# Spreading dt and u by broadcast reads, drives on GpSimd, decay in PSUM and half-row scans in a Mamba, attention and expert kernel

## The chip, the cores and the metric

The kernel runs on one core of a Trainium2 chip. The metric is the device time of one execution in microseconds, the median of several; less is better. Engines are named as in the profile: PE is TensorE, DVE VectorE, ACT ScalarE, POOL GpSimd, SP SyncE, which here only issues transfers.

## The reference

For each of 8 batches (64 channels, T = 1024 tokens) three layers follow each other: a selective scan (Mamba) with group norm and residual, causal attention of 8 heads of width 8, and a mixture of 8 experts, of which each token takes two. The part that the change is about:

```python
dt = jax.nn.softplus(dt_low @ W_dt + b_dt)      # [B, T, 128]
dA = jnp.exp(dt_t[..., None] * A)               # A: 128 x 16 states
dBx = dt_t[..., None] * B_t[:, None, :] * x_t[..., None]
h = dA * h + dBx                                # a recurrence over the 1024 tokens
y = jnp.einsum('bdn,bn->bd', h, C_t)
...
att = jnp.einsum('bqhd,bkhd->bhqk', q, k) * scale   # then causal softmax, times v
```

## The kernel before

A software pipeline runs over the batches. `pipeline` (L466) calls each engine's `program` for 12 turns, here turn 0 to 11; in a turn each part works on another batch: `c` the first half of the Mamba layer, `p` its end and the q and k projection, `b` the attention, `f` its projection and the experts. A full turn, with all of them, is turn 4 to 8. The order of each engine's work is written out by hand. Batches wait for each other by counting semaphores (`Signal`, L29).

A turn has two phases. The **score phase** is `for s in range(NSCORE)`: 48 steps of q times k (L1198, plus a mask product L1202) into two pairs of PSUM banks, and a row maximum on DVE over each (L926), so that the softmax can subtract it. q and k stand as three bf16 parts, so a product contracts 72 rows: `q_stack[0:9 * DH]`. Between these steps, at numbers in the tables `beside`, stands the dense work of `c` and `p`: the projections (L1106), the last folds of the scan, norms.

The **round phase** is `for s, units, turns in ROUNDS`: 28 rounds. From the fifth on each round has one of 24 attention steps: 4 products of k and q (`weigh`, 75 rows: the row maximum comes in as three more rows), 4 exponentials on ACT (L801), and the products with v (`add_values`). `TURNS` puts the experts of `f` into the rounds. `UNITS_IN` puts the scan of `c` there.

The scan has the 128 channels x 16 states as 16 chunks of 128 rows (8 channels times 16 states), each 1024 tokens long. Each chunk needs dt and u = dt * x of its 8 channels on 128 rows. Before, ACT and POOL split both into three bf16 parts in the score phase (`high`, `mid`, `less_high`, `less_mid`; L728, L732, L627, L632), SP copies them into `dt_rows` and `u_rows`, and PE replicates them with a 0/1 matrix, half a row at a time, into PSUM (L1236). ACT makes decay = exp(dt A) from there into SBUF (L762), DVE makes drive = u B (L979) and scans the whole row of 1024 (L970), POOL multiplies the state by C (L660), and PE sums the states (`fold_round`, L1126). Five PSUM banks are a ring for dt, u, scores, heads and experts, in order of use:

```python
ACC = 4
RING = (0, 1, 5, 6, 7)
...
read_by, batch, count = bank_read(users[place - len(RING)], c, b, f)
pe.wait_ge(read_by.sem, read_by.at(batch, count))
```

SP issues everything on one queue in program order, with its waits in between. At the end of the score phase and the start of the round phase that is: the parts of dt and u, t1, the parts of q and k, then it waits for the maxima (`max_t`, L962), writes them to memory and reads them back (L561, L564), and then loads the stacks of the next batch (L580) when attention has done with them.

## Time and profile before

| | |
|---|---|
| median of 3 runs (lowest to highest) | 1631.68 us (1628.54 to 1634.04) |
| profiled execution, its span | 1626.1 us, 1624.0 us |
| PE, DVE, ACT, POOL busy | 1260.7, 1171.9, 704.3, 512.2 us |
| TensorE clock granted, mean | 0.761 of full |
| DMA queue of the kernel | 25776 packets, 53.73 MB |

Busy is the time in which at least one instruction of an engine runs; PE's ends are modelled. The clock is 1 for 2.4 GHz and 0.5 for 1.2 GHz; a mean between them says how the time is split.

### The profile page before, as it was taken

The page shows a single profiled execution, that of the slowest core. Times are in us where ns is not written, and L with a number is a line of the kernel's source. Part 1 is how long each engine was busy: PE and PEld are TensorE (multiplying, and loading weights), DVE is VectorE, ACT ScalarE, POOL GpSimd, SP SyncE. Part 2 cuts the span into 40 slices and gives each one's busy share as a digit, 9 for nine tenths or more (in the row PEclk, how much of TensorE's full clock was granted, in tenths as well). Part 3 has the DMA queues.
Part 4 walks back from the last instruction along what each step waited for, and adds up shares of the span by engine and source line. Part 5 has one row for each costly group of instructions (what it writes and reads, how often), then busy time and mean ns, then how long its engine had stood idle before and what let it go on. Part 6 is the DMA issues. An engine that isn't in the chain of part 4 may idle for free. (4 is left out here: it accounts for less than half of the span.)

```text
span 1624.0 us, 17597 instructions
## 1 busy us (share of the span) xinstructions
PE 1260.7 (78%) x6388; PEld 499.9 (31%) x6388; DVE 1171.9 (72%) x1388; ACT 704.3 (43%) x1298; POOL 512.2 (32%) x272
## 2 busy tenths in 40 slices
PE   2455346888888987888887987888888988899894
PEld 1111111323233333333333323333233324433433
DVE  3396398787678968887679867887688867348345
ACT  1423322347434762376335642476326631460470
POOL 2454454344334332342243333342144321000000
PEclk9567556659966998589867997599758985695696
DMA  1100320021202111201211120201220120020000
GB/s 38 45 1 13 83 53 13 7 68 30 55 8 68 30 32 38 67 1 30 62 29 45 30 50 19 68 10 23 47 61 14 30 49 17 19 51 21 3 14 7
DMA packets 25863, 54.87 MB, mean 34 GB/s; under 512 B 8531, under 2 KB 8919, under 8 KB 23448
## 3 DMA queue, kind: packets, MB, share of 16 engines
q1 hardware_dynamic: 25776, 53.73, 14.6%
q8 instruction: 51, 0.84, 0.2%
q14 instruction: 36, 0.29, 0.1%
HBM read 28.15 MB, written 12.98 MB: 25 GB/s over the span
## 5 line engine op out<-in xcount | busy, mean ns | idle before, releaser
L926 DVE TENSOR_REDUCE row_max<-ps 128x1 f32<-128x768 f32 (+7 forms) x384 | 355.9, 952 | 142.2 <-PE ps L1202 139.6
L660 POOL TENSOR_TENSOR read<-state,c_rep 128x1024 f32<-128x1024 f32 x128 | 303.9, 2374 | 466.2 <-DVE state L970 450.6
L801 ACT ACTIVATE probs<-ps 128x512 f32<-128x512 f32 (+3 forms) x768 | 329.5, 496 | 144.7 <-PE ps L1305 86.5
L970 DVE TENSOR_TENSOR_SCAN state<-decay,drive 128x1024 f32<-128x1024 f32 x128 | 357.1, 2790 | 1.8 <-POOL read L660 1.1
L1198 PE MATMUL ps<-k_stack,q_stack 72*128 72x512 bf16 (+3 forms) x768 | 280.6, 456 | 83.2 <-DVE row_max L926 64.3
L1302 PE MATMUL ps<-q_stack,k_stack 75*128 75x512 bf16 (+3 forms) x768 | 222.8, 353 | 32.7 <-DVE drive L979 17.8
L979 DVE TENSOR_TENSOR drive<-ps,b_rep 128x512 f32<-128x512 f32 x256 | 169.6, 676 | 105.7 <-PE ps L1236 105.0
L762 ACT ACTIVATE decay<-ps,a_scale 128x512 f32<-128x512 f32 x256 | 175.3, 696 | 116.8 <-DVE state L970 100.1
L1236 PE MATMUL ps<-dt_rows,pick 96*128 96x512 bf16 x256 | 120.5, 471 | 96.9 <-DVE drive L979 69.5
L1317 PE MATMUL ps<-probs,v_aug 128*32 128x512 f32 (+3 forms) x1536 | 177.4, 536 | 4.1 <-ACT acc_sb L790 1.6
L1198 PEld LDWEIGHTS ps<-k_stack,q_stack 72*128 72x128 bf16 x768 | 73.8, 116 | 274.2 <-DVE row_max L926 171.4
L1302 PEld LDWEIGHTS ps<-q_stack,k_stack 75*128 75x128 bf16 x768 | 76.2, 102 | 245.4 <-ACT probs L801 89.4
L1202 PE MATMUL ps<-mask_q,ident_bf 128*128 128x128 bf16 x512 | 137.7, 278 | 0.0
L1236 PE MATMUL ps<-u_rows,pick 96*128 96x512 bf16 x256 | 120.8, 472 | 19.9 <-DVE attn L996 5.5
L1305 PE MATMUL ps<-mask_k,ident_bf 128*128 128x128 bf16 x512 | 110.4, 235 | 0.0
L597 POOL TENSOR_TENSOR ln_s<-ln_s,minus_half 128x8 f32<-128x8 f32 x16 | 26.3, 1643 | 262.2 <-DVE ln_s L904 262.2
L1202 PEld LDWEIGHTS ps<-mask_q,ident_bf 128*128 128x128 bf16 x512 | 65.2, 127 | 62.2 <-issue 54.2
L1236 PEld LDWEIGHTS ps<-dt_rows,pick 96*128 96x128 bf16 x256 | 27.4, 107 | 161.3 <-DVE drive L979 104.2
L1061 DVE TENSOR_TENSOR moe<-ps,gate_e 128x512 f32<-128x512 f32 x64 | 43.8, 685 | 44.9 <-PE ps L1286 44.9
L1126 PE MATMUL ps<-read,fold 128*32 128x512 f32 x512 | 74.6, 683 | 0.8 <-POOL read L660 0.8
L1106 PE MATMUL ps<-xc,w_bc 128*128 128x512 f32 x64 | 57.8, 1015 | 22.4 <-ACT b_rep L719 18.2
L1286 PE MATMUL ps<-w_expert,xn_t 96*128 96x512 f32 x128 | 69.3, 653 | 0.8 <-ACT decay L762 0.8
(169 smaller groups left out, 1281.6 us busy)
## 6 DMA issues: line engine op xcount, KB each, us to landing
q_stack<-q_parts_dram SPq DMA_DIRECT2D x48, 192.0 KB
k_stack<-k_parts_dram SPq DMA_DIRECT2D x48, 192.0 KB
dt_rows<-read SPq DMA_DIRECT2D x96, 64.0 KB, 2.0
u_rows<-read SPq DMA_DIRECT2D x96, 64.0 KB, 2.0
k_parts_dram<-read SPq DMA_DIRECT2D x40, 128.0 KB, 2.4
q_parts_dram<-read SPq DMA_DIRECT2D x24, 128.0 KB, 2.3
xs<-in_x SPq DMA_DIRECT2D x8, 256.0 KB, 3.5
residual<-in_x SPq DMA_DIRECT2D x8, 256.0 KB, 9.6
```

The lines of the kernel that those rows point to most:

```text
L660: pool.tensor_tensor(read[:, k % (2 * NG), :], state[:, k % 2, :], c_rep[:, :], ALU.mult)\
L762: act.activation(decay[:, k % 2, halves(h)], bank_of(("dt", k2)), ACT.Exp, scale=a_scale[:, j:j + 1])\
L801: act.activation(probs[:, e % (2 * QUAD), 0:w], bank_of(("scores", e))[:, 0:w], ACT.Exp, scale=SCALE).then_inc(exped.sem, 1)
L926: dve.tensor_reduce(row_max[:, i, h0:h0 + nh], scores[:, :, 0:P * (i + 1)], AX.X, ALU.max, negate=True).then_inc(row_maxed.sem, 1)
L970: dve.tensor_tensor_scan(state[:, k % 2, :], decay[:, k % 2, :], drive[:, k % 3, :], 0.0, ALU.mult, ALU.add).then_inc(scanned.sem, 1)
L979: dve.tensor_tensor(drive[:, k % 3, halves(h)], bank_of(("u", k2)), b_rep[:, halves(h)], ALU.mult)\
L1198: last = pe.matmul(ps[:, bank, 0:w], q_stack[0:9 * DH, h0 + hh, tokens(i)], k_stack[0:9 * DH, h0 + hh, h * BANK:h * BANK + w], start=True, ...
L1202: last = pe.matmul(ps[:, bank, w - P:w], ident_bf[:, :], mask_q[:, :], start=False, stop=True)
L1236: return pe.matmul(bank, pick[:, q, :, :].rearrange("p n e -> p (n e)"), rows[:, g, halves(k2 % 2)], start=True, stop=True)
L1302: last = pe.matmul(bank[:, 0:w], k_stack[0:KQ, head, tokens(j)], q_stack[0:KQ, head, lo:lo + w], start=True, stop=not diagonal)
L1305: last = pe.matmul(bank[:, 0:P], ident_bf[:, :], mask_k[:, :], start=False, stop=True)
L1317: last = pe.matmul(ps[GW * hq:GW * (hq + 1), ACC, lo:BANK], v_aug[:, j, quad * QUAD + hq, :], probs[:, (QUAD * s + hq) % (2 * QUAD), 0:BAN ...
```

## The change

- dt and u are stored to memory once a batch (512 KB each) and read back with a stride of zero over the states: each load of 256 KB puts 8 channels of half a row on 128 rows. The casts, the subtractions, `dt_rows`, `u_rows`, the matrix `pick` and 64 matmuls a batch go away. 64 loads a batch come in, on SP, 8 u and 6 dt of them ahead of the rounds, the others between them.
- The 16 scans of 1024 become 32 of 512: all chunks for the first half, then for the second, which starts from the last column that POOL has copied to `carry`.
- The drives move from DVE to POOL; the first six of a batch are made in the score phase, then each stands one place ahead of a read, six units early.
- ACT writes decay into PSUM banks 0 and 1; they leave the ring, which has three banks now. The turns up to the router have banks 2 and 3 (`TURN_BANK`).
- The score and weigh products contract all 128 rows. Rows 75 to 127 of `q_stack` are zero; rows 72 to 74, which hold the maxima later, are zeroed with each stack by a load.
- Seven of the eight folds stand in the rounds, one in the next score phase, where there were four and four. The first quad's stacks are loaded between the later scan loads.

```diff
-        dt_rows = sb("dt_rows", [96, NG, T], BF16)
-        u_rows = sb("u_rows", [96, NG, T], BF16)
...
+        DT_SLOTS, U_SLOTS, DRIVE_SLOTS, STATE_SLOTS, READ_SLOTS = 6, 8, 8, 4, 12
+        dt_rep = sb("dt_rep", [P, DT_SLOTS, BANK])
+        u_rep = sb("u_rep", [P, U_SLOTS, BANK])
+        drive = sb("drive", [P, DRIVE_SLOTS, BANK])
+        state = sb("state", [P, STATE_SLOTS, BANK])
+        read = sb("read", [P, READ_SLOTS, BANK])
+        carry = sb("carry", [P, NJ])
...
+                dve.memset(q_stack[64:P, :, :], 0.0).then_inc(zeros_set, 1)
...
-        UNITS_IN = (2, 2, 2, 1, 0, 2, 2, 0, 2, 1, 2, 1, 1, 1, 2, 1, 0, 0, 1, 1, 2, 1, 1, 2, 0, 1, 0, 1)
-        FOLDS = ((0, 0, 13), (0, 1, 13), (1, 0, 18), (1, 1, 19))
+        UNITS = NH * NJ
+
+
+        UNITS_IN = (2, 2, 1, 1, 1, 1, 1, 1, 1, 1, 2, 1, 1, 1, 1, 1, 1, 1, 1, 1, 1, 1, 2, 1, 1, 1, 1, 1)
+        FOLDS = ((0, 0, 6), (0, 1, 8), (0, 2, 11), (0, 3, 15), (1, 0, 18), (1, 1, 22), (1, 2, 25))
...
+        DRIVES_AHEAD = 6
...
-        RING = (0, 1, 5, 6, 7)
+        DECAY = (0, 1)
+        RING = (5, 6, 7)
...
+                    def load_rows(u, rows, slots, arrived):
+                        h, _, j = unit_of(u)
+                        slot = nth(c, u) % slots
+                        src = (dt_dram if rows is dt_rep else u_dram)[c.number, j * CH:(j + 1) * CH, halves(h)]
+                        sp.dma_start(rows[:, slot, :], src.unsqueeze(0).to_broadcast([NS, CH, BANK]))\
+                          .then_inc(arrived[slot].sem, 16)
+
+                    def load_dt(u):
+                        if nth(c, u) >= DT_SLOTS:
+                            sp.wait_ge(decayed.sem, nth(c, u) - DT_SLOTS + 1)
+                        load_rows(u, dt_rep, DT_SLOTS, dt_in)
+
+                    def load_u(u):
+                        if nth(c, u) >= U_SLOTS:
+                            sp.wait_ge(driven.sem, nth(c, u) - U_SLOTS + 1)
+                        load_rows(u, u_rep, U_SLOTS, u_in)
...
+                        for n in range(U_SLOTS):
+                            load_u(n)
+                        for n in range(DT_SLOTS):
+                            load_dt(n)
...
+                    for n in range(UNITS):
+                        if c and n + U_SLOTS < UNITS:
+                            load_u(n + U_SLOTS)
+                        if c and n + DT_SLOTS < UNITS:
+                            load_dt(n + DT_SLOTS)
+                        if p and 0 <= n - STACKS_AT < 6:
+                            load_stack(0, n - STACKS_AT)
...
+                    def drive_unit(u):
+
+                        h, _, j = unit_of(u)
+                        if u == 0:
+                            pool.wait_ge(b_copied.sem, b_copied.at(c, 1))
+                            pool.wait_ge(xc_ready.sem, xc_ready.at(c, 1))
+                            pool.wait_ge(z_ready.sem, z_ready.at(c, 1))
+                        pool.wait_ge(u_in[nth(c, u) % U_SLOTS].sem, landed(c, u, U_SLOTS))
+                        if u >= DRIVE_SLOTS:
+                            pool.wait_ge(scanned.sem, scanned.at(c, u - DRIVE_SLOTS + 1))
+                        pool.tensor_tensor(drive[:, u % DRIVE_SLOTS, :], u_rep[:, nth(c, u) % U_SLOTS, :],
+                                           b_rep[:, halves(h)], ALU.mult).then_inc(driven.sem, 1)
...
+                        if u >= READ_SLOTS:
+                            pool.wait_ge(folded.sem, folded.at(c, (u - READ_SLOTS) // NG + 1))
+                        pool.wait_ge(scanned.sem, scanned.at(c, u + 1))
+                        if h == 0:
+                            pool.tensor_copy(carry[:, k:k + 1], state[:, u % STATE_SLOTS, BANK - 1:BANK])\
+                                .then_inc(carried.sem, 1)
+                        pool.tensor_tensor(read[:, u % READ_SLOTS, :], state[:, u % STATE_SLOTS, :],
+                                           c_rep[:, halves(h)], ALU.mult).then_inc(read_out.sem, 1)
...
+                            if u + DRIVES_AHEAD < UNITS:
+                                drive_unit(u + DRIVES_AHEAD)
+                            read_unit(u)
...
+                        slot = nth(c, u) % DT_SLOTS
+                        act.wait_ge(dt_in[slot].sem, landed(c, u, DT_SLOTS))
+                        act.activation(banks(DECAY[u % 2]), dt_rep[:, slot, :], ACT.Exp,
+                                       scale=a_scale[:, j:j + 1]).then_inc(decayed.sem, 1)
...
+                    def scan(u):
+
+                        h, k, _ = unit_of(u)
+                        dve.wait_ge(decayed.sem, decayed.at(c, u + 1))
+                        dve.wait_ge(driven.sem, driven.at(c, u + 1))
+                        if u >= STATE_SLOTS:
+                            dve.wait_ge(read_out.sem, read_out.at(c, u - STATE_SLOTS + 1))
+                        if h:
+                            dve.wait_ge(carried.sem, carried.at(c, k + 1))
+                        dve.tensor_tensor_scan(state[:, u % STATE_SLOTS, :], banks(DECAY[u % 2]),
+                                               drive[:, u % DRIVE_SLOTS, :], carry[:, k:k + 1] if h else 0.0,
...
+                        pe.wait_ge(read_out.sem, read_out.at(batch, NJ * h + NG * (q + 1)))
...
-                                last = pe.matmul(ps[:, bank, 0:w], q_stack[0:9 * DH, h0 + hh, tokens(i)],
-                                                 k_stack[0:9 * DH, h0 + hh, h * BANK:h * BANK + w],
+                                last = pe.matmul(ps[:, bank, 0:w], q_stack[:, h0 + hh, tokens(i)],
+                                                 k_stack[:, h0 + hh, h * BANK:h * BANK + w],
```

What the edit does to the order is best seen on three engines. First POOL in a full turn. Before, at the end of the score phase and in the rounds (L627, L632 are the subtractions, L597 and L508 the norm, L642 the last part of q and k, L660 the reads):

```order
L627 TENSOR_TENSOR decay<-read 128x1024
L597 TENSOR_TENSOR ln_s<-ln_s,minus_half 128x8
L508 TENSOR_TENSOR xn<-xcen,ln_s 128x512
L627 TENSOR_TENSOR decay<-read 128x1024
L632 TENSOR_TENSOR read<-decay,read 128x1024 x2
L642 TENSOR_TENSOR read<-read 128x1024
L660 TENSOR_TENSOR read<-state,c_rep 128x1024 x16
```

And now the same place (L670 is a drive, L688 the copy of the last column, L690 a read, L632 and L513 the norm, L700 the last part of q and k):

```order
L649 TENSOR_TENSOR read<-read,residual 64x1024
L670 TENSOR_TENSOR drive<-u_rep,b_rep 128x512 x2
L632 TENSOR_TENSOR ln_s<-ln_s,minus_half 128x8
L513 TENSOR_TENSOR xn<-xcen,ln_s 128x512
L670 TENSOR_TENSOR drive<-u_rep,b_rep 128x512 x4
L700 TENSOR_TENSOR read<-read 128x1024
L670 TENSOR_TENSOR drive<-u_rep,b_rep 128x512
L688 COPY carry<-state 128x1
L690 TENSOR_TENSOR read<-state,c_rep 128x512
```

POOL has two products a half unit in the rounds where it had half a one, and a read waits behind the drive of six units later.

Next SP at the start of the rounds. Before:

```order
L561 DMA max_parts_dram<-max_t 24x1024
L564 DMA q_stack<-max_parts_dram 3x8192
L580 DMA q_stack<-q_parts_dram 24x4096
L580 DMA k_stack<-k_parts_dram 24x4096
```

Now (L541 is a broadcast read, L585 and L588 are the maxima):

```order
L541 DMA u_rep<-u_dram 128x1x512 x8
L541 DMA dt_rep<-dt_dram 128x1x512 x6
L568 DMA t_dram<-t 128x512
...
L585 DMA max_parts_dram<-max_t 24x1024
L588 DMA q_stack<-max_parts_dram 3x8192
L541 DMA u_rep<-u_dram 128x1x512
L541 DMA dt_rep<-dt_dram 128x1x512
```

The ninth load of u stands behind the maxima's way to memory and back.

Last DVE at the start of the rounds, before (a scan is printed as SCALAR_TENSOR_TENSOR here):

```order
L951 TENSOR_TENSOR max_parts<-max_rest,max_parts 128x8x8
L979 TENSOR_TENSOR drive<-ps,b_rep 128x512 x2
L962 COPY max_t<-ps 24x1024
L979 TENSOR_TENSOR drive<-ps,b_rep 128x512
L970 SCALAR_TENSOR_TENSOR state<-decay,drive 128x1024
L979 TENSOR_TENSOR drive<-ps,b_rep 128x512 x2
```

And now:

```order
L998 TENSOR_TENSOR max_parts<-max_rest,max_parts 128x8x8
L1021 SCALAR_TENSOR_TENSOR state<-ps,drive 128x512 x2
L1009 COPY max_t<-ps 24x1024
L1021 SCALAR_TENSOR_TENSOR state<-ps,drive 128x512 x3
L1084 TENSOR_TENSOR t<-t_back,ps 128x512
```

The drives are gone from DVE, and two half scans stand ahead of the copy of the maxima.

## Rows read from the trace of the kernel before

**Rows 1.** The page: span, and DVE's busy time
```profile
span 1624.0 us, 17597 instructions
...
PE 1260.7 (78%) x6388; PEld 499.9 (31%) x6388; DVE 1171.9 (72%) x1388; ACT 704.3 (43%) x1298; POOL 512.2 (32%) x272
```

**Rows 2.** Windows: length, busy of PE, PEld, DVE, ACT, POOL (x instructions), clock, DMA
```profile
428.00:503.00 75.00, 60.80 (x256) 24.96 (x254) 56.39 (x73) 22.39 (x23) 24.60 (x13) 0.73 0.22 50
503.00:604.00 101.00, 88.61 (x548) 35.97 (x548) 84.53 (x99) 65.17 (x140) 39.12 (x17) 0.90 0.13 28
...
1139.00:1217.00 78.00, 65.55 (x255) 25.98 (x252) 56.31 (x70) 21.78 (x22) 24.37 (x13) 0.67 0.22 49
1217.00:1318.00 101.00, 86.42 (x542) 34.30 (x542) 85.08 (x100) 66.02 (x141) 37.95 (x17) 0.90 0.10 24
...
1389.00:1459.00 70.00, 64.97 (x448) 29.94 (x448) 24.96 (x51) 45.66 (x108) 1.64 (x1) 0.87 0.12 25
1459.00:1512.00 53.00, 45.78 (x176) 18.51 (x176) 45.62 (x53) 0.00 (x0) 0.00 (x0) 0.53 0.11 26
```

**Rows 3.** Waits of the whole span: us, times, longest
```profile
POOL read L660 <- DVE state L970: 450.6, 120, 13.1
...
DVE row_max L926 <- PE ps L1202: 139.6, 138, 3.7
...
DVE drive L979 <- PE ps L1236: 105.0, 73, 30.9
```

**Rows 4.** Single lines and tiles: duration ns min/median/max, first and last start
```profile
L970 DVE TENSOR_TENSOR_SCAN state<-decay,drive x128: 2269/2292/4315, 67.7 to 1315.0; 128x1024 f32<-128x1024 f32 x128
...
L1021 DVE TENSOR_TENSOR gate_e<-gate_e,gate_m x8: 224/604/822, 547.5 to 1599.8; 128x64 f32<-128x64 f32 x8
...
L979 DVE TENSOR_TENSOR drive<-ps,b_rep x256: 652/675/693, 65.5 to 1314.3; 128x512 f32<-128x512 f32 x128
...
L1022 DVE TENSOR_TENSOR_SCAN gate_e<-expert_start,gate_e x8: 291/291/292, 548.4 to 1600.1; 128x64 f32<-128x64 f32 x8
...
L762 ACT ACTIVATE decay<-ps,a_scale x256: 668/687/771, 64.2 to 1314.2; 128x512 f32<-128x512 f32 x128
...
L627 POOL TENSOR_TENSOR decay<-read x16: 2112/2119/2121, 48.1 to 1198.7; 128x1024 f32<-128x1024 f32 x16
```

**Rows 5.** Groups of instructions by form: busy us, mean ns, idle before
```profile
L970 DVE TENSOR_TENSOR_SCAN state<-decay,drive 128x1024 f32<-128x1024 f32 x128 | 357.1, 2790 | 1.8 <-POOL read L660 1.1
L660 POOL TENSOR_TENSOR read<-state,c_rep 128x1024 f32<-128x1024 f32 x128 | 303.9, 2374 | 466.2 <-DVE state L970 450.6 <-DMA k_parts_dram<-read 13.2 <-PE ps L1126 2.4
...
L1198 PE MATMUL ps<-k_stack,q_stack 72*128 72x512 bf16 x384 | 195.7, 553 | 60.3 <-DVE row_max L926 57.2
...
L1302 PE MATMUL ps<-q_stack,k_stack 75*128 75x512 bf16 x384 | 131.7, 407 | 22.2 <-ACT decay L762 11.8 <-DVE drive L979 9.2 <-DMA q_stack<-max_parts_dram 0.8
...
L597 POOL TENSOR_TENSOR ln_s<-ln_s,minus_half 128x8 f32<-128x8 f32 x16 | 26.3, 1643 | 262.2 <-DVE ln_s L904 262.2
...
L508 POOL TENSOR_TENSOR xn<-xcen,ln_s 128x512 f32<-128x512 f32 x8 | 8.3, 1042 | 0.6
...
L1383 POOL MEMSET const-float32-0.0<- 128x1 f32 x1 | 0.1, 101 | 0.3 <-issue 0.3
```

**Rows 6.** Timeline of SP, 678 us on: start us, us
```profile
681.61 0.32 SPq L561 DMA_DIRECT2D max_parts_dram<-max_t  x1
683.22 0.26 SPq L564 DMA_DIRECT2D q_stack<-max_parts_dram  x1
```

**Rows 7.** DMA: the page's queue, tiles u_rows and xs, window 4.9 to 6.9 us
```profile
q1 hardware_dynamic: 25776, 53.73, 14.6%
...
L539 SPq DMA_DIRECT2D u_rows<-read x96: 507/590/593, 50.7 to 1212.5; - x96
...
DMA to landing us min/median/max: 3.4/3.9/4.3
...
q1 hardware_dynamic: 267, 0.13, 23.1%
```

## What the change will do to the time

> **What bounds the kernel now.** I read the page first. No engine is busy over 78% of the span and the page's DVE is at 72% [rows 1], so the share says nothing yet. The kernel alternates two phases on one program counter per turn, so I cut the span at the first row maximum and the first half decay of each turn and asked for busy time by stretch. In a full turn the score phase takes 75 to 78 us with DVE busy 56 us of it, and the round phase about 101 us with DVE busy 84.5 us, ACT 65 us, POOL 38 to 39 us; the five full turns run from 428 to 1318 us, 890 us, 178 each [rows 2], of which the first and the last stand there. The reader is to see that DVE is the fullest compute engine in the round phase, that it is not full in the score phase, and that TensorE's granted clock is 0.67 to 0.73 in the score phase and 0.90 in the round phase.
>
> Then the waits [rows 3]. In the score phase DVE waits for scores: 139.6 us in eight turns, 17.4 a turn, which is nearly all of its idle time there. In the round phase DVE waits for the replicating matmul (105.0 us) and POOL waits for scans (450.6), so DVE's own list sets the pace of the rounds. The last view is durations [rows 4, 5]: a scan of 1024 takes 2269 ns at least, 2790 ns in the mean and up to 4315. Another DVE instruction with both inputs in SBUF shows it too: the 64-element compare of L1021 takes 224 ns or up to 822. L979, whose one input is in PSUM, stays within 652 to 693 ns though POOL mostly runs beside it.
>
> **Round phase, DVE.** 32 drive products of 675 ns go away: 21.6 us. 16 scans of 2790 ns (44.6 us) become 32 half scans. A half scan is priced from L1022, 64 elements in 291 ns, and the shortest scan: slope (2269 - 291) / 960 = 2.06 ns an element, so 291 + 448 x 2.06 = 1.21 us, 38.8 us for 32. That assumes that the wait for POOL is gone with decay in PSUM, as L979 suggests; with it the pair costs 2.8 and the sum 44.6. DVE's list falls from 84.5 to about 57 us (63 at the other end).
>
> The Trainium skill (SBUF: State Buffer, "Who interferes with whom") says that a DVE instruction with two SBUF inputs and a GpSimd instruction that reads SBUF lock each other out for a whole instruction. By that rule the trace agrees; the sum would be the same by it.
>
> What is left to lose beside POOL are the gates, about ten DVE instructions with both inputs in SBUF in one row, of which L1021 shows up to 0.6 us of loss. With a POOL that is nearly full I charge 4 us: three to four of its instructions of 1.2 us, after which POOL itself has run out of scans to read.
>
> **Round phase, POOL.** It gets 32 drive products of 128x512 and 32 half reads in place of 16 whole ones. A whole read takes 2374 ns in the mean, half of it is 1.19; the only 128x512 product on POOL is L508 with 1.04 us (one input broadcast) [rows 5]. I take 1.22 us with the gap to the next, 1.04 and 1.3 being the ends. The 16 carry copies are at least the 0.10 us of a 128x1 memset; I take 0.15. Six drives are done in the score phase, where POOL has room (24 of 75 us busy, and the four subtractions of 2.12 us are gone).
>
> The start matters. The SP queue first issues 8 u and 6 dt loads, then waits for the maxima: before, the write of max_t was issued 3.6 us into the phase and its reading back at 5.2 [rows 6]. Now two half scans (2.4 us) stand where two drives (1.4) stood, so SP comes to the ninth u load at about 6.5 us. With 0.59 us of issue and 3.9 to landing [rows 7] POOL can make drive 8 at 11 us, and read 2 is queued behind it. From there 24 drives and 30 reads x 1.22 = 66, 14 copies 2, one L597 1.6: 81 us. With the gates' 4 and the last read before the next phase's last fold, 3: 88 us. ACT's list stays (32 decays of 0.69 us, 65 us in all) and is below that, DVE's 57 too. TensorE loses 64 matmuls. So POOL, not DVE, sets the rounds: **101 becomes 88**; ends 80 (1.04 us each, no stall) and 100.
>
> The Trainium skill (GPSIMD Engine Reference, "Engine selection") speaks against the move: elementwise work is about twice as slow there as on VectorE. The trace agrees (1.2 against 0.68 us).
>
> **Round phase, DMA.** 64 loads of 256 KB and two stores of 512 KB a turn are new. The page's queue moved 53.73 MB in 14.6% of 16 engines' span, which is 53.73 / (0.146 x 1624 x 16) = 14.2 GB/s an engine, 227 on 16: 1.15 us a load. A window with the load of conv_rows, a broadcast read too (128 KB from one row), shows 0.13 MB at 23.1%: 18 GB/s an engine, 0.93 us. At 1.15 the 50 loads of a round phase take 58 us plus 10 for what was there, under 88; issue takes 50 x 0.59 = 30 us of SP. A dt slot is refilled six units ahead, some 15 us, and landing takes 3.9. Hidden, unless a load costs about 1.9 us or more (below).
>
> **Score phase.** The zero rows add no columns. TensorE is busy 61 us of 75; the same 512-column score matmul takes 553 ns here and 407 in the rounds, at clocks of 0.7 and 0.9 [rows 5]. In the last score phase, scores alone, TensorE is busy 46 of 53 us and the clock is 0.53; in the round phase ahead of it, 65 of 70, it is 0.87 [rows 2]. So busy time alone does not tell the two apart; what does differ is that the former has mostly matmuls of 72 rows, and the latter many of 128. No row shows a score matmul on 128 rows. Bounds: nothing gained (75), or DVE's list of 56 and little more (60). If the clock comes to that of the rounds, TensorE's 61 us shrink by 407/553 to 45, under DVE's 56, and I keep about half of DVE's waits since the products still stand between scores: **76 becomes 66**. Three rounds of folds less at its start and 4 casts less on ACT help the same way.
>
> The Trainium skill (TensorE: Matmul & The Clock Gate, "What's actually happening") has the clock follow how busy the engine is, and a weight load cost by columns alone; it names no rows. By that the padding does nothing, and this phase stays at 75: the second case below.
>
> **First and last turns.** Turn 1: u is ready at 48.1 us (L627 starts), the first decay at 64.2 [rows 4, 5]; now a store of 512 KB at 227 GB/s (2.3), nine issues (5.3) and a landing (3.9) stand there, 59.6: 5 us less, and its rounds stay about as long (POOL now, 70 us). Turn 2: the chain of casts and subtractions is gone, 7 less. Turn 3: 8 less in the score phase, 2 more in the rounds, which had no experts. Turns 9 and 10 have scores without scans: 8 and 3 less, and 2 more each for a ring of three banks where there were five. Turn 11 stays.
>
> **Sum.** 890 - 5 x (66 + 88) = 120; 5 + 7 + 6 + 8 + 3 - 4 = 25; together 145 off the profiled execution's 1626.1 us: 1481. The median of the runs shown is 1631.68, 0.3% above it: **1485 us**.
>
> **The rivals.**
> - Clock unmoved (chance 0.20). For: busy time is what the rows show best. Against: 0.53 at 46 of 53 us busy. Score phases keep 10, 5 times, and 8 + 8 + 3: 1545 us.
> - The rounds stay near 100 us (0.13): PE waits in its queue for reads before each fold, experts share three banks with scores, gates wait for POOL. For: 8 experts and 96 scores through three banks. Against: ACT had 36 us of slack in 101. 5 x 12: 1545 us.
> - Both go well (0.13): score phase 61, rounds 82 (POOL products near 1.04 us). 5 x 11 more: 1425 us.
> - Slower (0.07): the broadcast loads set the pace. 50 are issued in the phase. For: 3.9 us to landing, if loads did not overlap. Against: 14.2 GB/s an engine as a mean over many small transfers. Break-even with the score gain kept is a phase of 178 - 66 = 112, (112 - 11) / 50 = 2.0 us a load, 1.9 with turns 1 to 3 counted; at 2.5 us the phase is 136, five turns lose 120, turns 1 to 3 about 50 each, and the time is 1626 + 120 + 150 - 25 = 1870 us.
> - The forecast itself: 0.45. The rest, 0.02, is a cancelling that leaves the time within 0.3%, about what a measurement can tell from no change.
>
> The range goes from the good case, 1425, less 10 for its own spread, to 1570, which takes in both cases at 1545 with 25 for their spread. Chances: faster 0.91, same 0.02, slower 0.07.
>
> **What the changed profile would show.** Half scans of 1.2 us with little spread; POOL busy over 85% of a full round phase with products of 1.2 us, DVE there under 65; score phases with a clock over 0.8 and a score matmul near 420 ns; u_rep loads landing in 3 to 5 us. Scans with a spread to 2.4 us would refute the PSUM step; a score clock of 0.7 the row step; landings over 10 us or POOL waiting for DMA the transfer step. The prediction is wrong low if POOL products take 1.4 us, or if the gates cost more than 10 us a turn.

## The result, and the profile after

The changed kernel takes 1643.68 us (median of 4 runs, 1642.44 to 1646.02) where the kernel before takes 1630.49 (4 runs beside it): a ratio of 1.0080, 95% interval 1.0058 to 1.0102. It is slower by 0.8%. The forecast of 1485 us is missed by 159, and the range with it.

The page of the profiled execution, for [rows 1]. The four groups shown are POOL's two products and the two halves of the scan on DVE (engine, operation, busy us, mean ns, idle before and its releaser):

```profile
span 1644.3 us, 17516 instructions
...
PE 1057.4 (64%) x5793; PEld 426.1 (26%) x5876; DVE 994.6 (60%) x1261; ACT 677.2 (41%) x1266; POOL 789.4 (48%) x748
...
L690 POOL TENSOR_TENSOR read<-state,c_rep 128x512 f32<-128x512 f32 x256 | 326.1, 1276 | 132.8 <-DVE state L1021 132.1
L670 POOL TENSOR_TENSOR drive<-u_rep,b_rep 128x512 f32<-128x512 f32 x256 | 325.7, 1277 | 31.0 <-DMA u_rep<-u_dram 31.0
...
L1021 DVE TENSOR_TENSOR_SCAN state<-ps,drive 128x512 f32<-128x512 f32 x128 | 152.8, 1213 | 168.6 <-ACT ps L812 125.5
L1021 DVE TENSOR_TENSOR_SCAN state<-ps,carry,drive 128x512 f32<-128x512 f32 x128 | 163.8, 1282 | 126.8 <-ACT ps L812 89.7
...
u_rep<-u_dram SPq DMA_DIRECT2D x256, 256.0 KB, 5.3
```

The single instructions cost what was forecast, or close to it: a half scan takes 1.25 us, a POOL product 1.28, a u load lands in 5.3. TensorE, DVE and ACT are busy for less time than before, POOL for more. Yet the span is 20 us longer. No engine is busy over 64%. Now the windows of [rows 2], the score and round phase of turn 5, then of turn 9, which has no scan (columns as there):

```profile
608.20:680.50 72.30, 50.46 (x222) 22.77 (x223) 55.46 (x71) 19.50 (x20) 23.25 (x15) 0.81 0.45 112
680.50:788.00 107.50, 78.41 (x505) 29.98 (x516) 68.93 (x85) 63.97 (x138) 75.19 (x74) 0.86 0.52 139
1330.70:1388.60 57.90, 40.78 (x202) 17.75 (x206) 51.81 (x67) 6.46 (x7) 10.04 (x6) 0.80 0.23 50
1388.60:1472.80 84.20, 69.35 (x449) 29.52 (x456) 25.60 (x54) 46.90 (x108) 1.64 (x1) 0.86 0.09 22
```

In the round phase DVE has 16 us less to do than before (69 us; the forecast was 57), and POOL 75 us as costed, but the phase is longer and every engine idles in it for 29 us or more. That is how a chain around several engines looks. Cut at the first and last row maximum of each turn, the span splits so (us; the first stretch holds turns 1 and 2, the last turn 11):

| stretch | before | after | moved | forecast |
|---|---|---|---|---|
| to turn 3's scores | 266.4 | 269.3 | +2.9 | -12 |
| turn 3, scores; rounds | 76.5; 85.5 | 76.4; 83.5 | -0.1; -2.0 | -8; +2 |
| turns 4 to 8, scores | 377.8 | 363.7 | -14.1 | -50 |
| turns 4 to 8, rounds | 512.4 | 537.8 | +25.4 | -70 |
| turn 9, scores; rounds | 69.7; 71.2 | 57.9; 84.2 | -11.8; +13.0 | -8; +2 |
| turn 10, scores; the rest | 51.4; 113.0 | 45.8; 125.7 | -5.6; +12.7 | -3; +2 |

The rounds lost what the score phases gained, and more. Two places of the trace tell how. First the chain of work in turn 6's score phase (start us, us, what; small issue gaps left out):

```profile
810.04 1.06 ACT state L755
...
811.17 2.34 POOL read L654
...
813.60 2.34 POOL read L658
815.93 0.53 POOL gn_v L643
...
817.10 1.20 ACT read L739
...
820.81 0.90 ACT b_rep L775
...
821.76 1.22 PE ps L1142
```

The group norm's power (L643) has its input at 809.7, but POOL makes softplus's sum and u first (L654, L658), and the ACT copy of b_rep and TensorE's next projection stand behind it. Before, POOL made the power first. The edit had moved it and the prediction had not looked at that place. Second, DVE, POOL, TensorE and ACT around the gates of turn 5 (timelines; in brackets idle before and its releaser):

```profile
726.49 1.17 DVE L1061 TENSOR_TENSOR gate_e<-gate_e,gate_m 128x64 f32<-128x64 f32 x1
727.70 2.60 DVE L1062 TENSOR_TENSOR_SCAN gate_e<-expert_start,gate_e 128x64 f32<-128x64 f32 x1
730.33 0.23 DVE L1064 SCALAR_TENSOR_TENSOR gate_e<-gate_e 128x64 f32<-128x64 f32 x1
...
727.67 1.26 POOL L690 TENSOR_TENSOR read<-state,c_rep 128x512 f32<-128x512 f32 x1
728.89 1.26 POOL L670 TENSOR_TENSOR drive<-u_rep,b_rep 128x512 f32<-128x512 f32 x1
...
733.16 1.28 DVE L1021 TENSOR_TENSOR_SCAN state<-ps,carry,drive 128x512 f32<-128x512 f32 x1
734.36 0.67 DVE L1101 TENSOR_TENSOR moe<-ps,gate_e 128x512 f32<-128x512 f32 x1
...
735.08 0.39 PE L1327 MATMUL ps<-q_stack,k_stack 128*128 128x256 bf16 x1 [6.46 <-DVE moe L1101]
...
735.62 0.39 ACT L850 ACTIVATE probs<-ps 128x256 f32<-128x256 f32 x1 [6.47 <-PE ps L1330]
```

The chain of 14 small gate operations takes 6.9 us, 4.2 before; its 64-element scan takes 2.60 us, which is 0.29 alone [rows 4]: it ends just behind the two POOL products that began with it (727.67 to 730.15). The first expert sits in one of three ring banks until the gates are done, the scores fill the other two, and TensorE and ACT stand 6.5 us.

### The profile page after: what moved, and what is told of

It is laid out like the page before. It is cut to its first block, busy times and chain, and to the rows that moved or that the text cites. A ratio compares the mean times of both kernels' runs of the same rounds, so it can differ in the third digit from the quotient of the medians.

```text
span 1644.3 us, 17516 instructions
## 1 busy us (share of the span) xinstructions
PE 1057.4 (64%) x5793; PEld 426.1 (26%) x5876; DVE 994.6 (60%) x1261; ACT 677.2 (41%) x1266; POOL 789.4 (48%) x748
## 4 chain that ended last, share of the span: by engine, by line
PE 30%; DVE 25%; issue 16%; POOL 15%; ACT 12%; DMA 1%; SPq 0%; POOLq 0%; DVEq 0%; ACTq 0%
DVE row_max L973 12%; POOL drive L670 6%; PE ps L1142 5%; POOL read L690 5%; PE ps L1342 5%; PE ps L1236 4%; PE ps L1327 4%; ACT probs L850 4%; PE ps L1162 3%; DVE moe L1101 2%; PE ps L1153 2%; DVE state L1021 2%; PE ps L1147 2%; ACT ps L812 2%; PE ps L1311 2%
## 5 line engine op out<-in xcount | busy, mean ns | idle before, releaser
L690 POOL TENSOR_TENSOR read<-state,c_rep 128x512 f32<-128x512 f32 x256 | 326.1, 1276 | 132.8 <-DVE state L1021 132.1
L670 POOL TENSOR_TENSOR drive<-u_rep,b_rep 128x512 f32<-128x512 f32 x256 | 325.7, 1277 | 31.0 <-DMA u_rep<-u_dram 31.0
L1327 PE MATMUL ps<-q_stack,k_stack 128*128 128x512 bf16 (+3 forms) x717 | 230.7, 360 | 136.3 <-DVE moe L1101 53.9
L1236 PE MATMUL ps<-k_stack,q_stack 128*128 128x512 bf16 (+3 forms) x736 | 225.1, 386 | 87.3 <-DVE row_max L973 76.9
L1021 DVE TENSOR_TENSOR_SCAN state<-ps,drive 128x512 f32<-128x512 f32 x128 | 152.8, 1213 | 168.6 <-ACT ps L812 125.5
L1021 DVE TENSOR_TENSOR_SCAN state<-ps,carry,drive 128x512 f32<-128x512 f32 x128 | 163.8, 1282 | 126.8 <-ACT ps L812 89.7
L812 ACT ACTIVATE ps<-dt_rep,a_scale 128x512 f32<-128x512 f32 x256 | 177.9, 697 | 147.4 <-DVE state L1021 136.0
L1327 PEld LDWEIGHTS ps<-q_stack,k_stack 128*128 128x128 bf16 x768 | 75.9, 102 | 404.4 <-ACT probs L850 229.5
L632 POOL TENSOR_TENSOR ln_s<-ln_s,minus_half 128x8 f32<-128x8 f32 x16 | 26.3, 1642 | 257.9 <-DVE ln_s L951 257.9
L1236 PEld LDWEIGHTS ps<-k_stack,q_stack 128*128 128x128 bf16 x768 | 68.0, 108 | 239.1 <-DVE row_max L973 173.8
L654 POOL TENSOR_TENSOR read<-drive,state 128x1024 f32<-128x1024 f32 x8 | 18.7, 2341 | 142.1 <-ACT state L755 142.1
L1240 PEld LDWEIGHTS ps<-mask_q,ident_bf 128*128 128x128 bf16 x512 | 57.9, 113 | 48.4 <-issue 26.5
L1105 DVE TENSOR_REDUCE moe_out<-moe 128x64 f32<-128x512 f32 x64 | 67.5, 1054 | 2.2
```

The lines of the kernel that those rows point to most:

```text
L670: pool.tensor_tensor(drive[:, u % DRIVE_SLOTS, :], u_rep[:, nth(c, u) % U_SLOTS, :], b_rep[:, halves(h)], ALU.mult).then_inc(driven.sem, 1)
L690: pool.tensor_tensor(read[:, u % READ_SLOTS, :], state[:, u % STATE_SLOTS, :], c_rep[:, halves(h)], ALU.mult).then_inc(read_out.sem, 1)
L812: act.activation(banks(DECAY[u % 2]), dt_rep[:, slot, :], ACT.Exp, scale=a_scale[:, j:j + 1]).then_inc(decayed.sem, 1)
L1021: dve.tensor_tensor_scan(state[:, u % STATE_SLOTS, :], banks(DECAY[u % 2]), drive[:, u % DRIVE_SLOTS, :], carry[:, k:k + 1] if h else 0.0, ...
L1236: last = pe.matmul(ps[:, bank, 0:w], q_stack[:, h0 + hh, tokens(i)], k_stack[:, h0 + hh, h * BANK:h * BANK + w], start=True, stop=not diag ...
L1240: last = pe.matmul(ps[:, bank, w - P:w], ident_bf[:, :], mask_q[:, :], start=False, stop=True)
```

## The experiments

Each kernel ran beside the kernel before on the same chip; ratios are to that. Phases are of the profiled runs; "full" is the mean of turns 4 to 8 (before: scores 75.6, rounds 102.5; after: 72.7 and 107.6). Each round from the fifth on has one attention step; the time from its first exponential to that of the next one, mean of turns 5 to 8, is called the step of its round.

**Rows of the contraction.** On the kernel before, the 128 rows alone, with the added rows zeroed as in the change; on the changed kernel the reverse, back to 72 and 75:

```diff
-  pe.matmul(..., q_stack[0:9 * DH, h0 + hh, tokens(i)], k_stack[0:9 * DH, ...
+  pe.matmul(..., q_stack[:, h0 + hh, tokens(i)], k_stack[:, ...
```

> The kernel before with the 128-row contraction alone: rows above 75 of the q stack zero, rows 72 to 74 zeroed by a load with each stack. Theory A (rows count for the clock, and what the changed kernel lost, it lost in the POOL order and in the three banks): score phases of full turns fall from 76 to about 68 us, of turns 9 and 10 by 12 and 7, 50 to 60 us off, about 1575 us. Theory B (rows do not count): 1630 us, the clock in the score phases stays at 0.67 to 0.73.

> The changed kernel with the score products on 72 rows and the weigh products on 75 again, nothing else changed (the zero loads stay). Theory A (rows count for the granted clock): the clock of the score phases falls from 0.8 to about 0.7 and of the rounds a little; score phases of turns 9 and 10 lengthen by 12 and 7 us, those of full turns by 2 to 4 us since they wait for the POOL chain in either case, 30 to 40 us in all, about 1680 us. Theory B (the clock follows how busy TensorE is, and the score phases changed because folds and casts left them): clock and time stay, 1644 us.

Measured: 1564.22 us, 0.9569 (0.9537 to 0.9602), and 1678.58 us, 1.0283 (1.0249 to 1.0318). Theory A in both. Of the first, the score phase and the rounds of turn 6 and the score phase of turn 9; then, of the second, the score phases of turns 6 and 9 (windows):

```profile
767.70:837.10 69.40, 50.40 (x247) 21.62 (x250) 55.03 (x69) 21.51 (x22) 24.16 (x13) 0.88 0.23 53
837.10:938.50 101.40, 85.38 (x542) 34.30 (x549) 85.28 (x103) 66.17 (x141) 38.67 (x17) 0.91 0.14 32
1279.70:1339.00 59.30, 42.00 (x226) 17.96 (x226) 52.05 (x67) 6.46 (x7) 11.11 (x7) 0.83 0.22 48
```
```profile
797.10:870.90 73.80, 55.60 (x226) 23.86 (x221) 55.25 (x70) 19.53 (x20) 23.24 (x15) 0.73 0.44 110
1350.10:1414.30 64.20, 50.34 (x206) 21.66 (x204) 52.24 (x67) 6.47 (x7) 10.04 (x6) 0.63 0.21 44
```

In the kernel before, with the same compute instructions but for their rows, the clock of a full score phase, which is between 0.67 and 0.73 [rows 2], rises to 0.88 (first row; 0.81 in turn 4), nearer to the level of 2.4 GHz, and TensorE's busy time in that of turn 6 from 65.4 to 50.4 us. The Trainium skill (TensorE: Matmul & The Clock Gate, "What's actually happening") has the clock follow how busy the engine was and names no rows; the measurement decides, rows count. One edit of the change, alone, is worth 4.3%. The rest of it costs all of that and 0.8% more. In the changed kernel the same rows are worth only half as much (1678.58 against 1643.68 us, 2.0 points of the ratio): a full score phase has 74.0 us without them and 72.7 with them, where it is 75.6 and 69.8 in the kernel before. So what the rest costs depends on what it is measured beside: 2.8% on 72 rows, 5.1 points on 128.

**POOL's order in the score phase.**

```diff
-  (c, add_softplus), (c, make_u), (p, group_inverse_root),
+  (p, group_inverse_root), (c, add_softplus), (c, make_u),
```

> The changed kernel with one line of POOL's list in its old place: the group norm's power (L643) ahead of the softplus sum and the product that makes u, as before, where the change puts it behind both. Theory A (the score phase of a full turn kept its length because the power now waits some 6 us for POOL, with it ACT's group norm, the copy of b_rep, PE's next projection and the scores): the power starts 6 us earlier in the phase, the phase goes from 73 to 67 us in the seven turns with both batches, 35 to 45 us off in all, about 1603 us. Theory B (the phase is held by DVE's and PE's hand over of scores whatever POOL does): the wait moves elsewhere, the time stays at 1644 within 5 us.

Measured: 1622.45 us, 0.9932 (0.9909 to 0.9954); full score phases 70.5 us. Theory A with half its size: 2.2 us off a full score phase, 7 us in turns 1 and 2.

**Banks of the ring.** Five banks in turns without a scan; and, in another kernel, the first four experts in bank 3, which is idle there (TensorE then waits until one is weighed before it makes the next):

```diff
+  def ring(c):
+      return RING if c else DECAY + RING
```
```diff
-  TURN_BANK = {..., ("router", 0): 3}
+  TURN_BANK = {..., ("router", 0): 3, **{("expert", n): 3 for n in range(4)}}
```

> The changed kernel, where turns without a scan (9 and 10 above all) get banks 0 and 1 back, so that their ring has five banks; in all other turns nothing changes. Theory A (three banks in place of five cost the rounds their overlap of TensorE, ACT and DVE): the round phases of turns 9 and 10 fall from 84 and 82 us to the 70 and 69 of before, 27 us off, about 1617 us. Theory B (they are longer for another reason, the 128 rows or the later experts): they stay, 1644 us.

> The changed kernel, in which the first four experts of a turn go to bank 3, idle there between the router and the second half's folds, and not to the ring of three, so that no score waits behind an expert that waits for the gates. Theory A (the ring of three ties TensorE to the gates): the attention step of round 14, 9.3 us where it was 2.9, comes down to about 5 and full round phases from 107.6 to about 103; seven or eight turns have experts, 25 to 30 us off, about 1616 us. Theory B (the ring does not decide in full turns, POOL's list or the decays' two banks do): under 5 us in all, 1640 us.

Measured: 1621.24 us, 0.9930 (0.9901 to 0.9958), and 1616.58 us, 0.9934 (0.9915 to 0.9953). Turn 9's rounds with five banks (window):

```profile
1390.90:1462.10 71.20, 62.61 (x450) 29.16 (x456) 25.67 (x54) 45.60 (x108) 1.64 (x1) 0.90 0.11 26
```

71.2 us, just as before. So 13 us of it were the two banks, with nothing else running but attention and experts. With the experts in bank 3 full rounds fall to 102.5 us and the step of round 14 from 9.4 to 1.7. Theory A in both. The Trainium skill (Perfetto Trace Analysis, "Optimizing Tensor Performance") asks that matmul groups rotate through different PSUM banks so that ACT's and DVE's reading overlaps the next group; here two banks fewer cost 13 of 71 us.

**Who paces the rounds.** Drives 8 of 512 columns wide, on POOL in the changed kernel and on DVE in the kernel before; broadcast loads 64 of 512 columns wide:

```diff
-  pool.tensor_tensor(drive[:, u % DRIVE_SLOTS, :], u_rep[...], b_rep[:, halves(h)], ALU.mult)
+  n = BANK if c.is_first else 8
+  pool.tensor_tensor(drive[:, u % DRIVE_SLOTS, 0:n], u_rep[...][0:n], b_rep[...][0:n], ALU.mult)
```

> The changed kernel, whose drives after the first batch are only 8 of 512 columns wide, so the output is not the reference's; every wait and transfer stays. It takes some 30 us of busy time a turn from POOL. Theory A (POOL is not what paces the rounds, its 75 of 107.6 us busy lie beside a chain of TensorE, ACT and DVE): the gates' chain gets back its 2.7 us and the start perhaps 2, full round phases 103 to 105 us, about 1620 us. Theory B (the step of the prediction, POOL's list with its reads behind drives sets the rounds): full round phases fall to 90 us or less, 1560 us or less.

> The kernel before, whose drives on DVE are only 8 of 512 columns wide after the first batch, so the output is not the reference's; every wait stays. It takes 32 x 0.45 = 14 us of busy time a turn from DVE and nothing from the other engines. Theory B (the prediction's first step: DVE's own list sets the pace of the rounds): full round phases fall by 14 us, from 102.5 to 88, seventy to ninety us off with the third turn, about 1550 us. Theory A (rounds follow a chain that goes round TensorE, ACT and DVE and is at 101 to 102 us whoever does the drives): full round phases 97 to 101 us, 1600 us or more.

> The changed kernel, whose broadcast loads bring only 64 of 512 columns after the first batch (the rest of a slot is old data, so the output is not the reference's); their number, order and waits stay. Theory A (transfers are hidden but for the ninth u load at the start of the rounds, which waits in the queue and not for bytes): within 5 us of the changed kernel, about 1640 us. Theory C (the rival that the broadcast loads hold the rounds, or slow other traffic): full round phases fall by 3 us or more, 1620 us or less.

Measured: 1600.54 us, 0.9834 (0.9814 to 0.9855), full rounds 101.3; 1590.51 us, 0.9765 (0.9720 to 0.9811), full rounds 97.9; 1642.11 us, 1.0072 (1.0049 to 1.0095), full rounds 106.9. The rounds of turn 6 of the second, for [rows 2] (window):

```profile
845.00:942.20 97.20, 84.81 (x547) 34.97 (x548) 73.96 (x101) 65.16 (x141) 38.53 (x17) 0.91 0.12 28
```

The 32 drives of a turn take 5.0 us for 21.7, but the 16 scans grow from 41 to 45 beside POOL's reads, so DVE has some 11 us less, and the phase gives 4.6 on the mean. DVE's list did not set the pace of the phase even before, or the 11 us would have come off. POOL loses a third of its list (a drive takes 0.23 us for 1.28), and full rounds fall by 6 us, not to 90. This gain lies in rounds 8, 9 and 14, whose steps go from 6.8, 4.0 and 9.4 to 3.5, 3.0 and 7.0. The part of round 14 is the gates' chain, 4.6 us for 6.9. The others are POOL's list: in turn 5 of the changed kernel POOL works almost without a pause from 12 to 50 us of the rounds; behind the gates it waits for scans. Neither list alone is the bound of the phase. The bytes of the loads are hidden from turn 2 on; their number, their order and the full loads of the first batch were left as they are and are not tested by this.

**Decay in SBUF, five banks in every turn.**

```diff
-  act.activation(banks(DECAY[u % 2]), dt_rep[:, slot, :], ACT.Exp, ...
+  act.activation(dt_rep[:, slot, :], dt_rep[:, slot, :], ACT.Exp, ...
```

> The changed kernel with decay in SBUF again: ACT writes it in place over the dt slot (a dt load therefore waits for the scan), still two units ahead at most, and banks 0 and 1 are back in the ring, which has five in every turn. Theory A (the banks that decay took cost more than the shared port does): half scans go from 1.21 and 1.28 us to 1.5 or so, round phases of turns 9 and 10 fall by 27 us in all, of full turns from 107.6 to about 101, near 1590 us. Theory B (with both inputs in SBUF the scans wait for POOL, which is busy 75 us of a round phase): half scans of 2 us and more in the mean, full round phases stay at 107 or grow, 1617 us or more.

Measured: 1716.60 us, 1.0546 (1.0525 to 1.0567): theory B, and more. Its scans (duration ns min/median/max) beside those of the changed kernel:

```profile
L1021 DVE TENSOR_TENSOR_SCAN state<-dt_rep,drive x128: 1185/2138/2626, 72.1 to 1370.3; 128x512 f32<-128x512 f32 x128
```
```profile
L1021 DVE TENSOR_TENSOR_SCAN state<-ps,drive x128: 1184/1223/1225, 70.4 to 1267.9; 128x512 f32<-128x512 f32 x128
```

With both inputs in SBUF the median of the first half's scans goes from 1.22 to 2.14 us. That the dt loads wait for scans here is not the cause: ACT waits for loads no longer than in the changed kernel (19.2 against 27.8 us in all). Most of the loss lies where POOL has a scan and little else to do beside it: 58 us up to turn 3's scores and 23 us in turn 3's rounds; the five banks give 13.1 us back in turn 9's rounds. The Trainium skill (SBUF — State Buffer, "Who interferes with whom") has such a DVE instruction and POOL's reads lock each other out; the trace agrees.

**Three fixes together** (POOL's order, five banks without a scan, experts in bank 3).

> The changed kernel with three edits together: POOL's power ahead of softplus and u, five ring banks in turns without a scan, the first four experts in bank 3. Theory A (they are separate losses): their gains add, 21 and 22 us as measured apart and some 28 for the experts, about 1572 us. Theory B (one gain eats the other, since a shorter score phase or round only moves the wait): 1590 us or more. The kernel before with the 128 rows alone took 1564 us: above that the rest of the change, with its worst losses mended, still does not pay.

Measured: 1586.31 us, 0.9760 (0.9709 to 0.9811), between the two: 72% of the sum of the three gains (0.032 of 0.044 in the ratio). Full rounds are 102.0 us, still those of before. What holds them there? Some of the steps that moved (us; the last two columns are two kernels described below):

| step of round | before | after | 3 fixes | 4 fixes | 4 fixes and POOL's rest after read 12 |
|---|---|---|---|---|---|
| 8 | 4.3 | 6.8 | 8.3 | 3.5 | 3.5 |
| 14 | 2.9 | 9.4 | 1.7 | 1.7 | 1.7 |
| 15 | 2.8 | 4.4 | 6.1 | 10.4 | 2.5 |
| 16 | 3.5 | 3.0 | 3.5 | 4.5 | 7.1 |
| full round phase | 102.5 | 107.6 | 102.0 | 102.9 | 97.3 |

**Round 8.** Two attempts, each on the three fixes: u loads 8 to 11 ahead of SP's wait for the maxima and the second norm's power one place earlier (five fixes); the folds later (four fixes). A third, on the four fixes, puts DVE's experts ahead of its scans.

```diff
-  FOLDS = ((0, 0, 6), (0, 1, 8), (0, 2, 11), (0, 3, 15), (1, 0, 18), (1, 1, 22), (1, 2, 25))
+  FOLDS = ((0, 0, 6), (0, 1, 10), (0, 2, 13), (0, 3, 16), (1, 0, 19), (1, 1, 22), (1, 2, 25))
```

> The kernel with three fixes (1586 us) with two more: SP issues u loads 8 to 11 ahead of its wait for the maxima, and POOL makes the second layer norm's power one place earlier. Theory A (round 8, 8.3 us where it was 4.3 before, is the layer norm behind POOL's list, which itself waits 4 us for the ninth u load): round 8 comes down to 4 or 5 us, full round phases from 102 to 98 or 99, turn 3 by a little, 15 to 25 us off, about 1565 us. Theory B (the wait moves to the next round): 1580 us or more.

> The kernel with three fixes (1586 us), whose folds 2 to 5 stand later: at rounds 10, 13, 16 and 19 for 8, 11, 15 and 18. Theory A (in round 8 TensorE stands about 4 us before the second fold, because POOL, at 2.6 us a unit, has not read unit 7, and the scores of the next rounds stand behind it): the step of round 8 comes from 8.3 to about 4.5 us, full round phases from 102 to 98 us, 20 to 25 us off, about 1564 us. Theory B (the early rounds wait for the layer norm or POOL's start, the fold only shows it): 1580 us or more, as with the early loads.

> The kernel with four fixes, in which DVE takes a round's experts ahead of its scans and not behind them. Theory A (rounds 14 to 22 are a lap: an expert holds one of three banks until DVE weighs it, which stands behind a scan, which stands behind ACT's decay, which stands behind the exponentials of the scores that want the bank): the steps of rounds 15 to 22 lose 1 to 1.5 us each where an expert is, full round phases fall by another 4 to 8 us, 25 to 50 us off the kernel with four fixes. Theory B (that lap is closed by ACT and TensorE alone, or a scan that comes later holds the decays): within 10 us of it, or slower.

Measured: 1585.54 us, 0.9744 (0.9697 to 0.9792); 1588.71 us, 0.9751 (0.9711 to 0.9791); 1615.61 us, 0.9914 (0.9887 to 0.9941). The early loads change nothing in the time (theory B), and the step of round 8 does not fall: in the profiled execution, of 1594.58 us, it is 10.8. The later folds do what was forecast for round 8, since TensorE stood there for POOL's read; the waits of the kernel with three fixes from 690 to 700 us show it:

```profile
PE ps L1165 <- POOL read L693: 4.1, 1, 4.1
```

But the gain is given back in round 15, so the expected 1564 us failed. Experts first makes it worse: round 22 takes 9.8 us; a shorter wait of the experts for DVE did not pay (theory B). The timeline of DVE in the kernel with four fixes says what round 15 waits for:

```profile
706.22 2.61 DVE L1065 TENSOR_TENSOR_SCAN gate_e<-expert_start,gate_e 128x64 f32<-128x64 f32 x1
708.87 2.48 DVE L1067 SCALAR_TENSOR_TENSOR gate_e<-gate_e 128x64 f32<-128x64 f32 x1
711.38 2.53 DVE L1068 SCALAR_TENSOR_TENSOR gate_e<-gate_e 128x64 f32<-128x64 f32 x1
```

The gates' first scan comes 42.0 us into the rounds now, and not 47.6, while POOL makes its products back to back up to 50 us, and the chain grows from 6.9 to 11.3 us.

**POOL rests during the gates**: after read 15 in the changed kernel and in the one with four fixes, there also with a gap in the scans and later experts; then after read 12, without and with the gap.

```diff
   if f and u == 4:
       inverse_root(1, f)
+  if c and f and u == 12:
+      pool.wait_ge(gate_chain.sem, gate_chain.at(f, 15))
```

> The changed kernel, whose POOL waits after read 15 until the gates' fourteen small DVE operations are done; nothing else is changed. Theory A (the gates' chain is stretched by POOL products that hold the port: it takes 6.9 us in the changed kernel, 4.2 before, 11 in the kernel with four fixes, where three of its 64-element operations take 2.5 us each): the chain falls to about 4.3 us, TensorE and ACT stand that much less before the first expert, 2 to 3 us off each of the five full turns, 1630 us. Theory B (what POOL loses by the wait it lacks later): no gain, 1640 us or more.

> The kernel with four fixes (1589 us) and the same rest of POOL during the gates. Theory A (the 7 us that the later folds gave back in round 15 are the gates' chain under POOL): the chain goes from 11 to about 4.5 us, the step of round 15 from 10.4 to 4 or 5, full round phases from 103 to 97 us, about 1560 us. Theory B (TensorE and ACT find another thing to wait for there, the scans behind the gates): 1580 us or more.

> The kernel with four fixes and POOL's rest, in which round 15 also has no scan (one more in round 19) and experts 1 to 3 come a round later, so that ACT's decays, TensorE's expert and the scores do not meet the gates. Theory A (what is left of the gates' stall is ACT's decay behind the scan behind the gates, and the expert behind the first one): another 2 us or so off each full round phase, about 1550 us. Theory B (the second half of the rounds is already full): within 5 us of the kernel with POOL's rest, or slower by the scan that comes later.

> The kernel with four fixes and POOL's rest (1576 us), which rests after read 12 and not after read 15. In the earlier one reads ran four units behind the scans, so POOL was still at work on reads 12 to 15 when the gates began, and their chain took 9.9 us. Theory A (the chain is long because of POOL's products, and full round phases wait for its end): the chain falls to 4 to 5 us, the step of round 15 from 9.5 to 4 or 5, full round phases from 101.5 to about 97 us, 1555 us. Theory B (the chain's end is not what the rounds wait for, or POOL's late reads hold them as much): the chain falls, the phases stay within 1 us, 1570 us or more.

> The same rest after read 12 in the kernel that also has no scan in round 15 and the experts 1 to 3 a round later (1569 us, full round phases 98.8 us). Theory A: the chain falls from 10 to 4 or 5 us, full round phases to 95 or 96 us, about 1550 us, under the 1564 us of the kernel before with 128 rows alone. Theory B: the second half of the rounds is bound by the lap of TensorE, ACT and DVE on three banks, what round 16 gains rounds 18 to 23 lose: 1565 us or more.

Measured: 1633.94 us, 1.0024 (1.0001 to 1.0046), chain 5 to 6 us, full rounds 106.3: theory A in part. 1575.79 us, 0.9655 (0.9630 to 0.9681), and with the gap 1569.08, 0.9620 (0.9595 to 0.9645), full rounds 101.5 and 99.1: the rest comes too late, the chain still takes 10 us, and neither theory is settled by it. After read 12: 1557.86 us, 0.9564 (0.9517 to 0.9611), full rounds 97.3, theory A; with the gap 1568.21 us, 0.9604 (0.9549 to 0.9660), rounds 99.3, theory B: on top of this rest the gap gives nothing. The gates' scan (L1067 there), and turn 6's rounds, in the kernel with the rest after read 12:

```profile
L1067 DVE TENSOR_TENSOR_SCAN gate_e<-expert_start,gate_e x8: 290/291/292, 532.4 to 1529.6; 128x64 f32<-128x64 f32 x8
```
```profile
825.50:924.20 98.70, 77.73 (x506) 30.69 (x516) 65.69 (x87) 63.78 (x138) 75.07 (x74) 0.86 0.57 152
```

Every gate chain takes 3.6 us, less than before the change. This kernel is the fastest measured and beats both kernels. It is not told apart from the kernel before with 128 rows alone: 0.9564 and 0.9569, the intervals lie over each other.

## Why the prediction was wrong

- **"DVE's own list sets the pace of the rounds"** is the step that failed. It was read from busy time (84.5 of 101) and from DVE's few idle reasons, although DVE did wait in every round phase, for the replicating product (105.0 us, [rows 3]). The narrow drives on DVE refute it: 11 us off the list, 4.6 off the phase. With it falls "POOL, not DVE, sets the rounds: 101 becomes 88": the POOL list was costed right (75 us busy, products of 1.28 where I took 1.22), but it was never the bound of the whole phase, only of a part of its first half. POOL was to be busy over 85% of a full round phase and was 70%; this was a sign that the prediction named itself. The likeliest case had 0.45.
- **DVE's list, 84.5 to 57**, came to 69, over the 65 that the prediction gave as a sign. The scans were to save 5.8 us and saved 0.9: the 2790 ns of [rows 5] are a mean over all turns, and in a full round phase the 16 scans took 40.8 us, 2.55 each, not 44.6. The small operations around them grew by 4.2 us beside a busier POOL (26.4 to 30.6). Since the list was not the bound, this did not decide the time.
- **The rival "rounds stay near 100"** named the right causes (three banks, gates, TensorE before the folds) and had 0.13, and it was priced as if the worst outcome was no gain. It allowed no loss: +5.1 us a full turn.
- **"2 more each for a ring of three banks where there were five"**, in turns 9 and 10: 13.0 and 12.7. The same banks gave 71.2 back. This term was guessed (turn 11 stayed, as forecast), while the waits of ACT and TensorE for each other stood in the trace.
- **The gates' 4 us**: the loss of the chain was 2.7 us, so the term was large enough, but it was put on POOL's list. It lies on the path of three engines, through the expert's bank. The step of round 14 grew by 6.5.
- **Score phase 76 to 66.** The clock rose and a 512-column score product took 461 ns (553 before, 420 forecast). The phase ended at 72.7. The rows alone gave 69.8, so the step was too large by 4, and POOL's moved power took 2.2 of the rest; it was in the order of instructions and I cited POOL's list without asking what its power releases.
- **Turn 3's score phase**, forecast 8 us shorter, kept its 76.4 us, though the rows alone bring it to 68.1 in the kernel before: around its start TensorE waits 7.8 us for POOL's last reads of the scan before.
- **Turn 1**: first decay at 69.7 us, not 59.6 (64.2 before). I counted nine issues and one landing, from the store of u on; the first dt load stands behind eight u loads that share the DMA engines with it, and lands at 68.3, 13.2 us after the first issue (55.1), where 9.2 were counted. The store itself landed at 55.0, where the sum had 50.4. A table load of ACT, 1.28 us, stands ahead of the first decay in both kernels and was not in the sum.
- **Right**: half scans of 1.21 (1.25), decay in PSUM free of POOL's lock, the transfers hidden behind turn 1, rows and clock. The mechanisms were there; what they are worth was read from the wrong bound.
- **Two sums of the rivals** are off: an unmoved clock gives 1485 + 50 + 19 = 1554 us by its own terms, not 1545, and the good case 1430, not 1425. The range and the failed step do not hang on this.
- **The case "slower"** (0.07) was held for the loads alone, at 1.9 us each. It came true by other means.

Open is how the 97.3 us that are left of a full round phase divide between the ring of three banks with a scan beside it, two banks of decay, and ACT's order; no run took these apart. Nor was it looked into why the rows alone give 69.8 us in a score phase and not 66. The move of the drives to POOL and the cut of the scans into halves were not run apart from each other either.

## What to carry to other kernels

Before you count a shortened list of one engine as gained time, make the list short in the old kernel and see what the phase does; here 11 us of DVE were worth 4.6. Take the mean of an instruction from the phase that you price, not from the whole span. A PSUM bank taken from a ring is a cost on the path, and it is best read in a turn that has little else. When an edit bundles several steps, run each alone: one of these (zero rows, 4.3%) was the whole gain, and the rest cost it again. Where a slow engine shares a port with a short dependent chain, let it rest there.

## What was not expected of the hardware

- The granted clock depends on the rows that a product contracts: 0.67 to 0.73 at 72 rows and 0.88 at 128 (0.81 in one of the five) in full score phases with otherwise the same compute instructions, worth 68 us of 1632.
- A small DVE operation with two SBUF inputs can take nine times its length beside a busy POOL: 0.29 us alone, 2.60 with POOL's products back to back, three of them in a row in one chain.
